# A hybrid eight-stage kernel: where the shared expert's chunks and the slot tables' weighing stand in the last feed-forward

## The reference, cut to what matters

```python
def _L1_ffn_ref(x, Wr, Wg, Wu, Wd, Sg, Su, Sd):
    xf = x.reshape(T, d)
    shared = jax.nn.silu(xf @ Sg) * (xf @ Su) @ Sd
    probs = jax.nn.softmax(xf @ Wr, axis=-1)
    topk_p, topk_i = jax.lax.top_k(probs, K)        # K = 2
    cw = jnp.zeros((T, n_exp), x.dtype).at[jnp.arange(T)[:, None], topk_i].add(topk_p)
    ...
    return (routed + shared).reshape(b, s, d)
```

## Time and profile before

| what | value |
| --- | --- |
| runs of the kernel | 4879.29 us median of 3 (4876.97 to 4886.81) |
| the profiled execution | 4889.6 us, span 4887.9 us |
| TensorE busy, share of the span | 3899.6 us, 80% |
| VectorE | 2850.8 us, 58% |
| GpSimd | 2449.1 us, 50% |
| ScalarE | 2215.5 us, 45% |
| granted TensorE clock, mean | 0.893 of full speed |

### The profile page before, as it was taken

How to read it: one execution, slowest core, us unless ns; L and a number is a source line. 1 busy time by engine, 2 the same in 40 slices (tenths; PEclk the granted TensorE clock), 3 DMA queues, 4 the chain that set the end, 5 groups by cost and what they waited for, 6 DMA issues and landing times.

```text
span 4887.9 us, 49289 instructions
## 1 busy us (share of the span) xinstructions
PE 3899.6 (80%) x15208; PEld 2245.9 (46%) x15210; DVE 2850.8 (58%) x4925; ACT 2215.5 (45%) x4073; POOL 2449.1 (50%) x2139
## 2 busy tenths in 40 slices
PE   6888888758965888799688869994895798888891
PEld 2333333346743555577333336663572333334571
DVE  5999999961125675211589962226435777664522
ACT  5665656521126776111566533333254455555251
POOL 5999999932212233211699954442356312222256
PEclk8999999969988999899799979995996799998896
DMA  4555666522210010222455531115054423322144
GB/s 149 161 160 158 163 158 157 155 78 69 99 66 18 18 35 22 84 88 70 127 164 161 151 112 45 45 42 162 27 152 124 110 41 46 47 29 60 35 143 132
DMA packets 310361, 471.88 MB, mean 97 GB/s; under 512 B 34506, under 2 KB 167350, under 8 KB 310026
## 3 DMA queue, kind: packets, MB, share of 16 engines
q1 hardware_dynamic: 276864, 388.61, 28.9%
q0 software_dynamic: 28992, 75.72, 5.5%
q10 hardware_dynamic: 4224, 4.19, 0.2%
HBM read 374.87 MB, written 97.10 MB: 97 GB/s over the span
## 4 chain that ended last, share of the span: by engine, by line
PE 37%; DVE 8%; issue 4%; ACT 4%; POOL 4%; DMA 2%; SPq 0%; DVEq 0%; POOLq 0%; ACTq 0%; another core or an unknown queue 0%
PE s_gate_up L2325 8%; PE s_result_sum L2341 4%; PE s_hidden_sum L1761 3%; PE s_result_sum L1772 3%; PE s_out_sum L3710 3%; PE s_shared L2981 2%; PE s_scores L3651 2%; DVE s_maxima L3335 2%; PE s_scores_T L3694 2%; DVE s_decay L370 2%; POOL s_gathered L1047 1%; PE s_shared L2991 1%; PE s_transposed L2315 1%; PE s_mid_transposed L2334 1%; PE s_y_sum L477 1%
## 5 line engine op out<-in xcount | busy, mean ns | idle before, releaser
L435 POOL TENSOR_TENSOR s_h<-s_dtu,s_bc 128x1024 f32<-128x1024 f32 x384 | 902.1, 2357 | 49.9 <-PE s_y_sum L477 37.8
L477 PE MATMUL s_y_sum<-s_h,identity 128*128 128x512 f32 x1536 | 779.7, 647 | 120.1 <-POOL s_h L444 107.3
L402 ACT ACTIVATE s_decay<-s_dt,s_A 128x512 f32<-128x512 f32 x768 | 499.5, 683 | 313.7 <-DVE s_h L377 306.7
L477 PEld LDWEIGHTS s_y_sum<-s_h,identity 128*128 128x128 f32 x1536 | 299.6, 205 | 564.1 <-issue 311.4
L2325 PE MATMUL s_gate_up<-s_w_gate_up,s_rowsT 128*128 x1168 | 414.5, 487 | 2.2 <-issue 2.0
L3507 ACT ACTIVATE s_weights_T<-s_scores_T 128x1024 f32<-128x1024 f32 (+3 forms) x384 | 292.8, 812 | 256.1 <-PE s_scores_T L3694 254.5
L3335 DVE TENSOR_REDUCE s_maxima<-s_scores 128x1 f32<-128x512 f32 (+3 forms) x463 | 296.9, 659 | 161.8 <-PE s_scores L3655 82.9
L444 POOL TENSOR_TENSOR s_h<-s_h,s_bc 128x512 f32<-128x512 f32 x288 | 365.6, 1270 | 19.1 <-DVE s_h L370 16.9
L2384 DVE TENSOR_TENSOR s_mid<-s_act,s_gate_up 128x128 f32<-128x128 f32 (+1 forms) x225 | 91.6, 407 | 446.5 <-ACT s_act L2357 424.5
L3555 POOL TENSOR_SCALAR_AFFINE_SELECT s_weights_T<-s_weights_T 128x256 f32<-128x256 f32 x256 | 103.2, 408 | 466.9 <-ACT s_weights_T L3507 464.3
L377 DVE TENSOR_TENSOR s_h<-s_decay,s_bc 128x512 f32<-128x512 f32 x480 | 315.5, 675 | 0.0
(11 more groups left out here) (538 smaller groups left out, 7641.9 us busy)
## 6 DMA issues: line engine op xcount, KB each, us to landing
s_bc<-s_bc_rows SPq DMA_DIRECT2D x384, 512.0 KB
sorted_results<-s_result SPq DMA_DIRECT2D x158, 128.0 KB
s_w_inter<-in_L_ffn_experts_inter SPq DMA_DIRECT2D x16, 1024.0 KB
s_w_exp_out<-in_L_ffn_experts_out SPq DMA_DIRECT2D x16, 1024.0 KB
s_queries<-parts_of_q SPq DMA_DIRECT2D x96, 128.0 KB
s_keys<-parts_of_k SPq DMA_DIRECT2D x96, 128.0 KB
results_by_token<-zeros SPq DMA_DIRECT2D x16, 512.0 KB, 6.0
s_pair<-results_by_token SPq DMA_DIRECT2D x16, 512.0 KB, 6.1
```

The source lines that it names most:

```text
L402: S.e.activation(self.decay[:, (2 * g + d) % 4, :], dt[q // self.passes % 2][:, at, :], ACT.Exp, scale=A[:, at, g % ns:g % ns + 1]).then_i ...
L435: G.e.tensor_tensor(self.h[r][:], dtu[q // self.passes % 2][:, at:at + 2, :], mid(self.bc[r][:, 0, :], 2), ALU.mult).then_inc(*self.fed.up())
L477: made = T.e.matmul(self.y[:, d, :], ident[:], self.h[r][:, d, :], start=False, stop=g % ns == ns - 1)
```

## The change

In the table, G takes no part any more: S weighs the comparison tile by tile, with the tile's number as a constant, 8 operations of 128x80 (128x40 in the capped mixture) for G's one. This holds in all four tables.

In the feed-forward, some of the shared expert's chunks are put between the fronts' chunks. In A the gate and up products of chunks 0 to 3 follow the logits of chunks 0, 2, 4 and 6, the down products of chunks 0 to 2 follow those of chunks 1, 3 and 5. In B, products of chunks 0 and 1 follow the logits of chunks 1 and 4, the down products those of 3 and 6. All chunks now go by S (copies of up and down banks) and G (product and sum). Behind the fronts, the down products of chunk c-1 stand behind the gate and up products of chunk c. The first two groups of the table stand ahead of the last chunk's down products, the other six behind them. `tensor_rank` stands after the second chunk behind the fronts. `xT` has 4 buffers in A; the planes get buffers of their own; up and down copies get a tile each. S copies the transposes of a chunk before it normalises the next. The loads of the experts' weights stand behind all the stores. V issues all the groups of the table right after the routing.

```diff
-    def gpsimd_group(self, g):
-        ...
-        G.e.tensor_tensor(self.tile[g % self.RING][:, :, 1, :], self.same[g % 2], last(self.K.iota[:, tiles], self.n),
-                          ALU.mult).then_inc(*self.by_tile.up())
+        first = tiles.start + (NT * i if self.planes else 0)
+        for k in range(self.GROUP):
+            made = S.e.activation(self.tile[g % self.RING][:, k, 1, :], self.same[g % 2][:, k, :], ACT.Copy,
+                                  scale=float(first + k))
+        made.then_inc(*self.by_tile.up())
...
+    if K.owed == "normed":
+        MULTIPLIED, FINISHED, TURNED = {0: 0, 2: 1, 4: 2, 6: 3}, {1: 0, 3: 1, 5: 2}, 4
+    else:
+        MULTIPLIED, FINISHED, TURNED = {1: 0, 4: 1}, {3: 0, 6: 1}, NC
+    INSIDE = len(MULTIPLIED)
...
         for c in range(NC):                                   # scalar()
-            if owed is not None and c + 2 < NC:
-                owed.scalar_square(c + 2)
+            turned_copies(c)
+            squares(c + 2)
+            if c in MULTIPLIED:
+                gate_and_up(MULTIPLIED[c], 0)
             if c + 1 < NC:
                 normalise(c + 1)
-            for k in range(DT):
-                ...
+            if c in MULTIPLIED:
+                gate_and_up(MULTIPLIED[c], 1)
+            if c in FINISHED:
+                outs(FINISHED[c], 0)
+                outs(FINISHED[c], 1)
         R.scalar_exp()
+        groups = iter(range(table.GROUPS))
+        for c in range(INSIDE, NC):
+            gate_and_up(c, 0)
+            gate_and_up(c, 1)
+            if c - 1 not in FINISHED.values():
+                outs(c - 1, 0)
+                outs(c - 1, 1)
+        for i in range(2):
+            table.scalar_group(next(groups))
+        outs(NC - 1, 0)
+        outs(NC - 1, 1)
+        for g in groups:
+            table.scalar_group(g)
...
+        for c in range(NC):                                   # gpsimd()
+            root(c)
+            if c - 2 in MULTIPLIED:
+                gate(MULTIPLIED[c - 2], 0)
+                gate(MULTIPLIED[c - 2], 1)
+            if c - 2 in FINISHED:
+                add(FINISHED[c - 2], 0)
+                add(FINISHED[c - 2], 1)
+            ln.gpsimd_factors(c)
...
+        for c in range(NC):                                   # tensor()
+            front(c)
+            if c in MULTIPLIED:
+                gate_and_up(MULTIPLIED[c])
+            if c in FINISHED:
+                outs(FINISHED[c])
+        groups = iter(range(table.GROUPS))
+        for c in range(INSIDE, NC):
+            gate_and_up(c)
+            if c - 1 not in FINISHED.values():
+                outs(c - 1)
+            if c == INSIDE + 1:
+                R.tensor_rank()
+        for i in range(2):
+            table.tensor_group(next(groups))
+        outs(NC - 1)
+        for g in groups:
+            table.tensor_group(g)
```

More of the change, by code:

```diff
@@ L1494, in gpsimd_place @@
     def gpsimd_place(self, c, bank):
-        for i, g in self.groups(c):
-            yield i + 1
-            self.table.gpsimd_group(g)
+        yield from ()
     def tensor_place(self, c, take):
@@ L2867, in vector @@
         table.vector_split()
[L2868 to L2873, removed]
-                R.vector_tiles()
[L2875 to L2889, removed]
+        for g in range(table.GROUPS):
+            table.vector_group(g)
+            if g == table.RING - 1:
+                R.vector_tiles()
+        table.vector_rows()
     def scalar():
@@ L2899, in scalar, with turned_copies, gate_and_up, outs @@
         pick = itertools.cycle(banks)
+        def turned_copies(c):
+            for k in range(DT):
+                f = next(pick)
+                S.wait_ge(*turned.at(DT * c + k))
+                S.wait_ge(*up_sum.at(FK * (c - TURNED) + FK - 1))
+                S.e.activation(xT[c % TURNED][:, k, :], f[:], ACT.Copy).then_inc(*xT_made.up())
+        def gate_and_up(c, f):
+            gb, ub = next(pick), next(pick)
+            S.wait_ge(*gate_sum.at(FK * c + f))
+            S.wait_ge(*mid_made.at(FK * (c - 2) + f))
+            S.e.activation(hs[c % 2][:, f, :], gb[:], ACT.Silu).then_inc(*gated.up())
+            S.wait_ge(*up_sum.at(FK * c + f))
+            S.wait_ge(*mid_made.at(FK * (c - 1) + f))
+            S.e.activation(up_copies[:, f, :], ub[:], ACT.Copy).then_inc(*up_copied.up())
+        def outs(c, i):
+            b = next(pick)
+            S.wait_ge(*out_sum.at(2 * c + i))
+            S.wait_ge(*added.at(2 * (c - 1) + i))
+            S.e.activation(out_copies[:, i, :], b[:], ACT.Copy).then_inc(*out_copied.up())
+        def squares(c):
+            if owed is not None and c < NC:
+                owed.scalar_square(c)
         if owed is not None:
@@ L2913, in scalar @@
-        R.scalar_exp()
[L2914 to L2933, removed]
+            if c in MULTIPLIED:
+                gate_and_up(MULTIPLIED[c], 1)
@@ L2935, in gpsimd, with root @@
+        for g in groups:
+            table.scalar_group(g)
     def gpsimd():
-        for c in range(NC):
+        def root(c):
             if owed is not None:
                 owed.gpsimd_root(c)
-            ln.gpsimd_factors(c)
[L2940 to L2950, removed]
@@ L2957, in tensor, with front @@
         T.wait_ge(*shared_here.at(0))
-        for c in range(NC):
+        def front(c):
             for k in range(DT):
```

81 lines of the change are left out of this document (41 added, 40 removed).

## The result

The kernel before took 4878.84 us (median of 4 runs) and the changed kernel 4840.57 us (median of 4, 4838.39 to 4845.29): a ratio of 0.9922, 95% interval 0.991 to 0.9934, or **38.3 us (0.8%) faster**. Forecast were 26.0 faster and 4853, with a range of 4836 to 4884. The profiled execution took 4845.29 us with a span of 4843.6.

What follows compares the result with a forecast made beforehand. Bound: T behind the fronts and in B's fronts, a loop of SP, transfer, V, G and S in A's fronts, G in the table. -5.9 - 0.8 - 23.7 + 4.4 = -26.0 us, giving 4853 (4836 to 4884).

Steps and rivals of the forecast that it cites:

- The tables: State-space table and capped mixture: S's weighing at 2.05 us a group for G's 2.93 gives -5.9 and -0.8 us.
- A's fronts: Feed-forward A, up to the last logits: 24.0 us a pair of chunks against 20.55, so +13.3 us.
- T becomes the bound here: A's fronts: T's work of 24.0 us a pair of chunks exceeds the old loop's 20.55 and sets the pace.
- I take it as hidden under 24.0: A's fronts: the next chunk's normalisation, store and planes, behind the first up bank's copy, fit within the pair's 24.0 us.
- Behind the fronts: After the last logits, T runs without gaps: 45.0 us in A, 62.4 in B, before the tail.
- The tails: End of A and of B: S weighs the table's groups while T is nearly idle, 26.0 us each.
- B: Feed-forward B: fronts +20.8 us, then 62.4 and a tail of 26.0, together 109.2 against 104.8, so +4.4.
- The copies ahead of the second normalisation: B's fronts: S copying first lets the first logits start some 3 us earlier, counted as 3.0.
- The clock did not stay up: Rival 1, fronts: products hold T at 2.4 GHz, a pair takes 17.2 us, total -42, 4837 us; chance 0.12.
- the products did not run at 1.2 GHz: Rival 3, fronts: products at 1.2 GHz throughout, 33.3 us a pair, total +26.7, 4906 us; chance 0.09.
- The small operations do overlap: Rival 2, tables: S's small operations don't overlap, 3.2 us a group, total +3.6, 4883 us; chance 0.11.
- S did hold the norm's chain: Rival 4, A's fronts: S waits for T's banks, growth some 45 us, total about +6; 0.08 including the unseen.

Runs made afterwards that it cites:

- experiment 1: Changed kernel with GpSimd's one operation of 128x640 a group put back in all four tables: 4856.99 us, ratio 0.9956 to the kernel before.
- experiments 4 to 6: Changed kernel with, in A's fronts, chunk 1 normalised earlier on S (4833.18 us); half of T's gate-and-up products (4837.25 us); G's sums cut to 16 columns (4835.81 us).
- experiment 3: Changed kernel with no shared chunk between the fronts of feed-forward B, all eight behind them: 4842.11 us, ratio 0.9924 to the kernel before.
- experiment 8: Changed kernel with G making the norm's factors ahead of the shared chunk's gated products and sums in B's fronts: 4832.32 us, ratio 0.9903 to the kernel before.

## Why the prediction was right, and where not

- *The tables.* Right. The group was put at 2.05 us and took 1.99; the state-space table gave 6.6 for 5.9, the capped mixture's 1.9 for 0.8, inside the bounds given. Only the weighing's worth in the tails was not seen (experiment 1).
- *A's fronts.* The size was near (+10.6 for +13.3), the mechanism was not, and that the size came near is luck. The step that failed is "T becomes the bound here", and with it "I take it as hidden under 24.0": chunk 1's normalisation behind the first up bank was not hidden. It held the loop 7.6 us. The three pairs of stores behind it took 22.3, 22.4 and 24.6 us for 20.6, 19.9 and 19.5, 9.2 more: G's work stretched V's sums, and in the last pair T's last set stood in the chain. The last front took 6.2 less, most of it by S copying first. In the middle of the fronts T was not the bound (experiments 4 to 6); it was at their start and for the last 18.5 us.
- *Behind the fronts.* The term that was mis-sized most. I charged 9.2 us for the first set and 3.69 for down products; T comes out of the fronts already at 2.4 GHz (logits in 1.96 us), and they took 6.96 in A (the first two 13.83 in B) and 3.45 back to back. That is 41.8 for 45.0 and 59.0 for 62.4: 6.6 of the 10.3 us by which the traces beat the forecast. The tails were right, 26.3 and 25.1 for 26.0.
- *B.* Fronts +21.0 for +20.8, but the terms differ, and that they cancel is luck. In the chain the second set took 6.98 for 9.2 and the down products 5.17 and 6.42 for 4.5, and the two waits behind G's gated products (5.2) were not foreseen; sets, down products and waits come to 32.9 for 27.4. The fronts that stand right behind products then gave back about 9.5 for 3.6. The copies ahead of the second normalisation gave 2.4 of the 3.0 counted (48.7 for 51.1 us without chunks). That the chunks are worth nothing there is shown by experiment 3.
- *The rivals.* The clock did not stay up throughout the fronts (0.75, 0.72), and the products did not run at 1.2 GHz throughout either (7.1 to 9.8 us a set, not 13.8). The small operations do overlap. S did hold the norm's chain, but 7.6 us behind the first set and 7.0 behind the last, where no later chunk waited for it, and not for all that was put in. Of the signs of being wrong, time in untouched stages showed, 8 of 44 us between the two executions, about half of it spread.

## What to carry to other kernels

Before an engine is called the bound because its work fills a period, look through which engine the chain runs: here a single copy put ahead of a step in a loop delayed the turns behind it, and the period looked like that of the busy engine. Halving that engine's work and finding the loop's stretch as long as ever settled it here. In-order queues want their order by what is ready first, stage by stage; the same swap won 6.8 us in one stage's fronts and lost 8.3 in the other's. Work taken out from beside a busy engine to make room comes back as a tail, so price the tail, and see whether halves of it fit under the other engine's products.

## What the runs showed that I had not expected

In B's fronts without chunks T was granted 1.2 GHz (0.50) for all of 48.7 us, and was busy for 43.2 of them: being busy did not get it the upper clock there. In experiment 8 the first front behind a set of wide products still runs at 2.4 GHz (logits in 1.96 us), and the second front in a row falls back, at both places (3.59 us, clock 0.50), with no pause in them longer than 0.8 us.
